# Gated products reordered across four engines, and probabilities scaled by VectorE instead of GpSimd, in a two-layer fp32 transformer kernel

## The chip, the core and the metric

The kernel runs on one core of a Trainium2 chip. The metric is the device time of one launch in microseconds (us). "Before" was timed three times. The engines go by the profile's names: PE (TensorE), DVE (VectorE), ACT (ScalarE), POOL (GpSimd), SP (SyncE, which here only issues DMAs).

## The reference

Eight sequences of 256 rows and 256 columns pass through one cross-attention over a context and then through a block of two layers, `x + tanh(g) * block(layernorm(x))`. One layer of the block, cut to what matters:

```
h = shift_token(x); q, k, v = split(h @ wqkv)          # 8 heads of 64
q, k = rotary_xpos(l2norm(q) * qs, l2norm(k) * ks)
sim  = (8 q) @ k.T over windows of 128 (own and previous), masked
o    = softmax(sim) @ v;  x = x + o @ wo
h = layernorm(shift_token(x)) * lg + lb
a, g = split(h @ w1 + b1)                               # 682 columns each
x = x + (a * gelu(g)) @ w2 + b2
```

All is fp32. Products with weights are made of three fp32r matmuls each, high by high, high by low and low by high part, so every right-hand tensor is split: a rounded copy (`u_hi`), and the remainder (`u_lo = u - u_hi`).

## The kernel before

After a first part (the cross-attention of the eight sequences, about the first 130 us) come 17 steps, s = 0 to 16. Step s does the attention of sequence-layer s and, in the same instruction streams, the feed-forward of sequence-layer s - 1; step 0 has attention only, step 16 feed-forward only. Steps 0 to 7 take layer 0, steps 8 to 15 layer 1; steps 0 and 8 also prepare weights and hold 44 narrow matmuls (L517). Each engine runs an order written out by hand, and counting semaphores tie the engines together; nothing is reordered at run time.

The feed-forward of a step has HC = 6 column chunks (5 of 128 and one of 42). For chunk c: PE `up(c)`; ACT `gelu(c)` (L830, L833); DVE `gated(c)` multiplies to `u_full[c % 4]` (L1139, semaphore `u_raw`); ACT `high_u(c)` rounds it (L839, `u_high`), but the last chunk's rounding is DVE's `high_last_u` (L1147), which waits until ACT has rounded the other five and then counts on the same semaphore; POOL `low_u(c)` forms the remainder (L1352, `u_done`). PE `down(n)`, n = 0 to 11 (two row tiles of six chunks), is the product with w2; the first six wait for `u_done`. Between chunks 3 and 4 POOL also adds the offset b2 to x1 (L1394, `xb_done`), which DVE reads only at L1260, late in the step.

The attention of a step, for each of eight heads: PE scores (L594, L600); DVE `row_min` (mask and row minimum, two instructions of 128x128 and 128x256, L1158); ACT `exps` (two ACTIVATEs with row sums, L858); DVE `row_sum` (reciprocal, L1164, `rl_done`); POOL `normalise` (two TENSOR_SCALARs over `pr`, L1370, `pn_done`); PE `tr_probs` (three transposes, L609 to L611); ACT `probs_T` (L864); PE `weighted` for each pair of heads (L623, L627); ACT `heads_out` (L869) and DVE `low_oT` (L1151). PE then transposes the next input (L415), finishes `down` and multiplies by wo (L422).

Earlier in the step DVE sums squares (`norms`, L1082), forms the low part of the feed-forward's input (`low_hT`, L1130), which `up(0)` waits for, and turns queries and keys (L1096 to L1126); POOL takes inverse square roots (L1341) and adds keys (L1346).

Before the first exponential of a step ACT loads another table (L922). In program order ACT does `gelu(4)`, `keys_T(1)`, `high_u(3)`, `gelu(5)`, the table load, `high_u(4)`, `exps(0)`, `exps(1)`; DVE does `gated(5)`, `high_last_u`, `row_min(0)`, `row_min(1)`, `row_sum(0)`, `row_min(2)`; PE does the first pair's scores, five downs, the second pair's scores, `tr_probs(0)`.

Of the kernel before, what the change touches and what calls it, by code (L numbers as in the profile page):

```python
# [18 lines left out]
P = 128  # L19
# [10 lines left out]
HEADS, DH = 8, 64  # L30
# [19 lines left out]
def build(nc, x, ctx_in, mask, g_xattn, g_ffn, Wq, bq, Wk, bk, Wv, bv, ln_gamma, ln_beta,  # L50
# [25 lines left out]
    with st:  # L76
# [99 lines left out]
        zeros_set, nhalf_set, tanh_done, prep_done = sem("zeros_set"), sem("nhalf_set"), sem("tanh_done"), sem("prep_done")  # L176
        touch_set, q1_done = sem("touch_set"), sem("q1_done")
        dve_passed, pool_passed = sem("dve_passed"), sem("pool_passed")
# [229 lines left out]
        def _(pe):  # L408
# [113 lines left out]
            def step(s, la, lf):  # L522
# [174 lines left out]
                if A:  # L697
# [8 lines left out]
                    for h in range(HEADS + 1):  # L706
                        if h in (0, 1, 3):
                            scores_own((h + 3) // 2)
                            scores_both((h + 3) // 2)
                        if h < HEADS:  # L710
                            tr_probs(h)
                        if isinstance(s, int) and s in (0, NB) and h == HEADS - 1:
                            bias_products(la)
                        downs(5 + min(5, (5 * h + 7) // 8))
                        if h and h % 2 == 0:
                            weighted(h // 2 - 1)
# [24 lines left out]
        def _(act):  # L741
# [68 lines left out]
            def step(s, la, lf):  # L810
# [100 lines left out]
                if lf is not None:  # L911
                    high_u(1)
                    gelu(3)
                    high_u(2)
                    gelu(4)
                if la is not None:
                    keys_T(1)
                if lf is not None:
                    high_u(3)
                    gelu(5)  # L920
                if la is not None:
                    A(table_touch[:, 1:2], table_touch[:, 0:1], ACT.Exp)  # L922
                if lf is not None:
                    high_u(4)
                if la is not None:
                    exps(0)
                    exps(1)
                    for h in range(HEADS):
                        if h + 2 < HEADS:
                            exps(h + 2)  # L930
                        if h >= 3 and h % 2:
                            heads_out((h - 3) // 2)
                        probs_T(h)
                    heads_out(PAIRS - 1)
                    if not (isinstance(s, int) and s == STEPS - 1):
                        evac_yT(s + 2)
# [7 lines left out]
        def _(dve):  # L944
# [131 lines left out]
            def step(s, la, lf):  # L1076
# [66 lines left out]
                def high_last_u():  # L1143
                    c, r = HC - 1, hrows[HC - 1]
                    dve.wait_ge(u_raw, HC * s)
                    dve.wait_ge(u_high, HC * s - 1)
                    V.tensor_copy(u[0][0:r, c, :], u_full[c % 4][0:r, :]).then_inc(u_high, 1)  # L1147

# [11 lines left out]

                def row_sum(h):
                    dve.wait_ge(e_done, T * (HEADS * s + h + 1))
                    wait(dve, pn_done, T * HEADS * s)
                    V.reciprocal(rl[:, h, :], ls[:, h, :]).then_inc(rl_done, 1)  # L1164

                A, F = la is not None, lf is not None
# [31 lines left out]
                if A:  # L1198
# [3 lines left out]
                    norms(1, 0)  # L1202
                    norms(1, 1)
                if F:
                    low_hT()
                if A:
                    scale_heads(0)
                    rotate_cos(1)
# [27 lines left out]
                if A:  # L1236
                    row_min(0)
                    row_min(1)
                    row_sum(0)
                    row_min(2)  # L1240
                    if start:
                        normalise_mid(NB - 1)
                    for h in range(HEADS):
                        if h + 1 < HEADS:
                            row_sum(h + 1)
                        if h + 3 < HEADS:
# [33 lines left out]
        def _(pool):  # L1280
# [51 lines left out]
            def step(s, la, lf):  # L1332
# [16 lines left out]
                def low_u(c):  # L1349
                    pool.wait_ge(u_high, HC * f + c + 1)  # L1350
                    r = hrows[c]
# [10 lines left out]
                def low_w2(l):  # L1362
                    for i, (full, high, low) in enumerate(pieces(l, False)[0:LAST_W2 - FIRST]):
                        pool.wait_ge(w_high, PIECES * l + FIRST + i + 1)
                        G.tensor_tensor(low, full, high.bitcast(F32), ALU.subtract).then_inc(w2_ready, 1)

                def normalise(h):
                    wait_apart(pool, pool_passed, (rl_done, HEADS * s + h + 1))
                    for t, (a, b) in enumerate(((0, P), (P, 3 * P))):
                        G.tensor_scalar(pr[:, h % NS, a:b], pr[:, h % NS, a:b], rl[:, h, t:t + 1], 1.0,  # L1370
                                        ALU.mult, ALU.mult).then_inc(pn_done, 1)

# [13 lines left out]
                if start:  # L1386
                    context_rstd(NB - 1)
                    rstd_x(2, NB - 1)
                if lf is not None:
                    for c in range(HC):  # L1390
                        if c == HC - 2:
                            pool.wait_ge(x1_done, s)
                            wait(pool, res_done, f)
                            G.tensor_tensor(x1b, x1[:], b2_bc[lf][:].unsqueeze(1).to_broadcast([P, T, D]),  # L1394
                                            ALU.add).then_inc(xb_done, 1)
                        low_u(c)
                if la is not None:
                    for h in range(HEADS):
                        normalise(h)
                if isinstance(s, int) and s in (0, NB):  # L1400
# [57 lines left out]
```

## Time and profile before

| what | value |
|---|---|
| median of the runs (range) | 833.61 us (833.32 to 834.94) |
| the profiled execution's own time | 832.07 us |
| its span, first to last instruction | 830.3 us |
| busy share PE, DVE, ACT, POOL | 88%, 65%, 58%, 53% |
| mean granted TensorE clock | 0.956 of full |
| one middle step (window 363.8 to 405.0 us), busy PE / DVE / ACT / POOL | 38.05 / 26.46 / 26.89 / 24.06 us of 41.2 |
| chain that ended last, share of the span | PE 46%, ACT 11%, DVE 11%, issue 10%, POOL 5% |

The chain follows the last instruction back to what released each one. PE is the busiest engine, but its modelled ends overlap, and its share says nothing of a single stretch: what a step can save is read from the waits inside it.

### The profile page before, as it was taken

How to read it: one execution, taken by the hardware profiler on the slowest of the kernel's cores; microseconds unless marked ns; L12 is line 12 of the kernel's file. 1: busy time of each engine (PE TensorE's matmuls, PEld its weight loads, DVE VectorE, ACT ScalarE, POOL GpSimd, SP SyncE). 2: the span in 40 equal slices, each digit the busy share in tenths (PEclk: the TensorE clock that was granted, in tenths of full speed). 3: DMA queues.
4: the chain of work that ended last, by engine and by line, in shares of the span. 5: the costliest groups of instructions: out<-in, count | busy, mean ns of one | idle time of the engine just before them, and what ended most of it. 6: DMA issues, size and time to landing. Idle time of an engine off the chain costs nothing.

```text
span 830.3 us, 17109 instructions
## 1 busy us (share of the span) xinstructions
PE 730.6 (88%) x4984; PEld 607.8 (73%) x4984; DVE 535.6 (65%) x1486; ACT 482.2 (58%) x1289; POOL 436.6 (53%) x592
## 2 busy tenths in 40 slices
PE   6898676989998989898988998899989899999867
PEld 5787554877777777777776877777777777777746
DVE  2899895384747474747575836666666666666632
ACT  2333424465757575757576655756575757575642
POOL 0433553473738383838382736747373737474622
PEclk9999975899999999999999988999999999999988
DMA  6444323261010101010101001010101010101000
GB/s 212 147 139 144 120 45 106 58 221 39 1 39 0 38 0 38 0 38 0 38 0 39 1 1 51 3 51 0 51 0 51 0 51 0 51 0 39 2 26 13
DMA packets 32786, 38.36 MB, mean 46 GB/s; under 512 B 8476, under 2 KB 22896, under 8 KB 32752
## 3 DMA queue, kind: packets, MB, share of 16 engines
q1 hardware_dynamic: 32752, 37.95, 14.2%
q8 instruction: 16, 0.26, 0.1%
q14 instruction: 18, 0.15, 0.1%
HBM read 29.55 MB, written 8.39 MB: 46 GB/s over the span
## 4 chain that ended last, share of the span: by engine, by line
PE 46%; ACT 11%; DVE 11%; issue 10%; POOL 5%; DVEq 1%; ACTq 0%; POOLq 0%
PE ps L422 26%; PE ps L623 4%; ACT pr L858 4%; PE ps L582 3%; ACT L922 2%; PE ps L609 2%; PE ps L600 2%; PE ps L594 2%; DVE ss L1082 2%; DVE turned L1096 2%; POOL rn L1341 1%; PE ps L627 1%; ACT pT L864 1%; POOL pr L1370 1%; PE ps L415 1%
## 5 line engine op out<-in xcount | busy, mean ns | idle before, releaser
L1370 POOL TENSOR_SCALAR pr<-pr,rl 128x128 f32<-128x128 f32 (+1 forms) x256 | 107.0, 430 | 78.7 <-DVE rl L1164 78.0
L858 ACT ACTIVATE pr<-sm,mn 128x128 f32<-128x128 f32 (+1 forms) x256 | 113.4, 445 | 30.2 <-DVE mn L1158 30.1
L422 PE MATMUL ps<-hT_hi,w_hi 128*128 128x256 f32 (+1 forms) x352 | 105.3, 299 | 5.4 <-DVE hT_lo L1130 5.4
L1158 DVE CUSTOM_DVE_ANT_0 sm<-ps,wmask 128x128 f32<-128x128 f32 (+1 forms) x256 | 79.9, 354 | 45.2 <-PE ps L600 39.9
L422 PE MATMUL ps<-hT_hi,w_lo 128*128 128x256 f32 (+1 forms) x352 | 100.4, 285 | 0.0
L422 PE MATMUL ps<-hT_lo,w_hi 128*128 128x256 f32 (+1 forms) x352 | 99.5, 283 | 0.0
L1341 POOL TENSOR_TENSOR rn<-ss,nhalf 128x16 f32<-128x16 f32 x32 | 96.7, 3022 | 2.7
L818 ACT ACTIVATE sqb<-ps 128x512 f32<-128x512 f32 x64 | 38.0, 595 | 95.0 <-PE ps L422 88.3
L422 PE MATMUL ps<-wqkv_hi,yT_hi 128*128 128x512 f32 x192 | 80.0, 417 | 7.7 <-DVE arena L1002 5.2
L1286 POOL TENSOR_SCALAR hrs<-hmv 128x2 f32<-128x2 f32 x16 | 3.1, 192 | 152.9 <-DVE hmv L1181 152.9
L1352 POOL TENSOR_TENSOR u_lo<-u_pair,u_hi 128x256 fp32r<-128x256 f32 x64 | 70.9, 1116 | 23.4 <-ACT u_hi L839 22.7
L422 PE MATMUL ps<-w_hi,u_hi 128*128 128x256 f32 x192 | 66.3, 345 | 16.6 <-POOL u_lo L1352 16.5
L422 PE MATMUL ps<-wqkv_lo,yT_hi 128*128 128x512 f32 x192 | 77.1, 402 | 0.0
L422 PE MATMUL ps<-wqkv_hi,yT_lo 128*128 128x512 f32 x192 | 77.0, 401 | 0.0
L422 PEld LDWEIGHTS ps<-hT_hi,w_hi 128*128 128x128 f32 (+1 forms) x352 | 66.9, 190 | 12.5 <-DVE hT_lo L1130 12.4
L830 ACT ACTIVATE gl<-ps,b_sb 128x256 f32<-128x256 f32 x80 | 37.9, 474 | 56.4 <-PE ps L422 55.4
L864 ACT ACTIVATE pT<-ps 128x384 f32<-128x384 f32 x128 | 61.5, 482 | 11.9 <-PE ps L611 10.5
L422 PEld LDWEIGHTS ps<-hT_lo,w_hi 128*128 128x128 f32 (+1 forms) x352 | 67.2, 191 | 0.0
L422 PEld LDWEIGHTS ps<-hT_hi,w_lo 128*128 128x128 f32 (+1 forms) x352 | 66.6, 189 | 0.0
L609 PE MATMUL ps<-ident,pr 128*128 128x128 f32 x128 | 42.2, 330 | 23.1 <-POOL pr L1370 21.8
L1151 DVE TENSOR_TENSOR oT_lo<-ps,oT_hi 128x256 fp32r<-128x256 f32 x64 | 27.1, 423 | 49.7 <-ACT oT_hi L869 48.1
L609 PEld LDWEIGHTS ps<-ident,pr 128*128 128x128 f32 x128 | 18.2, 142 | 52.8 <-POOL pr L1370 44.8
(150 smaller groups left out, 2137.5 us busy)
## 6 DMA issues: line engine op xcount, KB each, us to landing
arena<-x SPq DMA_DIRECT2D x16, 256.0 KB, 3.4
ystream<-arena SPq DMA_DIRECT2D x16, 256.0 KB, 2.0
y_next<-ystream SPq DMA_DIRECT2D x16, 256.0 KB, 2.8
y_res<-ystream SPq DMA_DIRECT2D x16, 256.0 KB, 2.7
arena<-L_ffn_w SPq DMA_DIRECT2D x6, 640.0 KB
arena<-ctx SPq DMA_DIRECT2D x8, 256.0 KB, 3.7
arena<-mask_BxSxS_ik SPq DMA_DIRECT2D x8, 256.0 KB, 2.7
xmid<-arena SPq DMA_DIRECT2D x8, 256.0 KB, 2.0
```

The costliest lines, as they stand in the source:

```text
L422: last = mm(out, lhsT(a), rhs(b), start=(start and i == 0), stop=(stop and i == 2))
L609: nc.tensor.transpose(b[:, 0:P], p[:, 2 * P:3 * P], ident[:])
L623: mm(b[j * DH:(j + 1) * DH, 0:S], vs[:, 0, h * DH:(h + 1) * DH], pT[:, h % 4, P:3 * P], start=True, stop=False)
L818: A(sqb[:, j * INNER:(j + 1) * INNER], bank(i + j), ACT.Square).then_inc(sq_done, 1)
L830: A(gl[:, c % 2, :], ps[:, 5 + c % 2, S:2 * S], ACT.Gelu, bias=b1_sb[:, lf, 1, c:c + 1]).then_inc(gl_done, 1)
L858: A(pr[:, h % NS, a:b], sm[:, h % NS, a:b], ACT.Exp, bias=mn[:, h, t:t + 1], scale=-1.0, accum_out=ls[:, h, t:t + 1]).then_inc(e_done, 1)
L864: A(pT[:, h % 4, :], bank(3 + h % 2)[:, 0:3 * P], ACT.Copy).then_inc(pT_done, 1)
L1151: V.tensor_tensor(oT[1][:, pair, :], bank(5 + pair % 2)[:, 0:S], oT[0][:, pair, :].bitcast(F32), ALU.subtract).then_inc(o_done, 1)
L1158: V.tensor_tensor_reduce(sm[:, h % NS, a:b], bank(h % SB)[:, a:b], wmask[:, a:b], 1.0, -NEG, ALU.add, ALU.min, mn[:, h, t:t + 1]).then_inc ...
L1341: G.tensor_tensor(rn[:, t, :], ss[:, t, :], nhalf[:], ALU.pow).then_inc(rn_done, 1)
L1352: G.tensor_tensor(u[1][0:r, c, :], u_full[c % 4][0:r, :], u[0][0:r, c, :].bitcast(F32), ALU.subtract).then_inc(u_done, 1)
L1370: G.tensor_scalar(pr[:, h % NS, a:b], pr[:, h % NS, a:b], rl[:, h, t:t + 1], 1.0, ALU.mult, ALU.mult).then_inc(pn_done, 1)
```

## The change

On DVE the reciprocal of the row sums is followed at once by the two multiplications of `pr`, and `normalise` leaves POOL. `high_last_u` no longer waits for ACT and has a semaphore of its own, `u_last`. ACT rounds chunks 3 and 4 before `gelu(5)` and the table load. POOL adds b2 after all six `low_u`. PE does two more downs ahead of `tr_probs(0)` and spreads the rest otherwise. On DVE `low_hT` moves ahead of the fourth `norms`. The diff without its line numbers and unchanged surroundings:

```diff
 # tensor
+                        if h == 0:
+                            downs(7)
                         if h < HEADS:
                             tr_probs(h)
...
-                        downs(5 + min(5, (5 * h + 7) // 8))
+                        downs(min(10, 7 + (h + 1) // 2))
 # scalar
                     gelu(4)
+                    high_u(3)
                 if la is not None:
                     keys_T(1)
                 if lf is not None:
-                    high_u(3)
+                    high_u(4)
                     gelu(5)
                 if la is not None:
                     A(table_touch[:, 1:2], table_touch[:, 0:1], ACT.Exp)
-                if lf is not None:
-                    high_u(4)
-                if la is not None:
                     exps(0)
 # vector, high_last_u
                     dve.wait_ge(u_raw, HC * s)
-                    dve.wait_ge(u_high, HC * s - 1)
-                    V.tensor_copy(...).then_inc(u_high, 1)
+                    V.tensor_copy(...).then_inc(u_last, 1)
-                def row_sum(h):
+                def scale_by_sum(h):
                     dve.wait_ge(e_done, T * (HEADS * s + h + 1))
-                    wait(dve, pn_done, T * HEADS * s)
                     V.reciprocal(rl[:, h, :], ls[:, h, :]).then_inc(rl_done, 1)
+                    dve.wait_ge(rl_done, HEADS * s + h + 1)
+                    for t, (a, b) in enumerate(((0, P), (P, 3 * P))):
+                        V.tensor_scalar(pr[:, h % NS, a:b], pr[:, h % NS, a:b], rl[:, h, t:t + 1], None,
+                                        ALU.mult).then_inc(pn_done, 1)
...
                     norms(1, 0)
+                if F:
+                    low_hT()
+                if A:
                     norms(1, 1)
-                if F:
-                    low_hT()
-                if A:
                     scale_heads(0)
 # vector, the loop over heads: row_sum becomes scale_by_sum in both places
 # gpsimd
                 def low_u(c):
-                    pool.wait_ge(u_high, HC * f + c + 1)
+                    if c < HC - 1:
+                        pool.wait_ge(u_high, (HC - 1) * f + c + 1)
+                    else:
+                        pool.wait_ge(u_last, s)
...
-                def normalise(h):
-                    wait_apart(pool, pool_passed, (rl_done, HEADS * s + h + 1))
-                    for t, (a, b) in enumerate(((0, P), (P, 3 * P))):
-                        G.tensor_scalar(pr[...], pr[...], rl[...], 1.0, ALU.mult, ALU.mult).then_inc(pn_done, 1)
...
                 if lf is not None:
                     for c in range(HC):
-                        if c == HC - 2:
-                            (wait x1_done, res_done; add b2 to x1)
                         low_u(c)
+                    add_offset()      # the same wait and addition
-                if la is not None:
-                    for h in range(HEADS):
-                        normalise(h)
```

## Rows read from the trace of the kernel before

**Rows 1.** timeline of PE, step 6: start, us, engine, line, operation [idle <-releaser]

```profile
377.66 0.38 PE L422 MATMUL ps<-hT_hi,w_hi 128*128 128x256 f32 x1 [0.23 <-DVE hT_lo L1130]
...
390.99 0.38 PE L422 MATMUL ps<-w_hi,u_hi 128*128 128x256 f32 x1 [1.03 <-POOL u_lo L1352]
...
391.54 0.49 PE L594 MATMUL ps<-kT,qT 64*128 64x128 f32 x4
...
393.54 0.33 PE L609 MATMUL ps<-ident,pr 128*128 128x128 f32 x1 [1.08 <-POOL pr L1370]
...
402.11 0.65 PE L623 MATMUL ps<-pT,vs 128*64 128x256 f32 x4 [0.18 <-DVE oT_lo L1151]
```

**Rows 2.** timeline of ACT, step 6

```profile
389.52 0.20 ACT L922 ACTIVATE table_touch<-table_touch 128x1 f32<-128x1 f32 x1
...
391.09 0.40 ACT L858 ACTIVATE pr<-sm,mn 128x128 f32<-128x128 f32 x1 [1.06 <-DVE mn L1158]
...
393.36 0.40 ACT L858 ACTIVATE pr<-sm,mn 128x128 f32<-128x128 f32 x1 [0.41 <-DVE mn L1158]
...
397.25 0.40 ACT L858 ACTIVATE pr<-sm,mn 128x128 f32<-128x128 f32 x1
...
398.72 0.49 ACT L864 ACTIVATE pT<-ps 128x384 f32<-128x384 f32 x1 [0.22 <-PE ps L611]
...
401.50 0.95 ACT L864 ACTIVATE pT<-ps 128x384 f32<-128x384 f32 x2
```

**Rows 3.** timeline of POOL, step 6

```profile
388.47 1.28 POOL L1394 TENSOR_TENSOR arena<-x,b_bc 128x512 f32<-128x512 f32 x1
390.11 1.51 POOL L1352 TENSOR_TENSOR u_lo<-u_pair,u_hi 128x256 fp32r<-128x256 f32 x2 [0.35 <-ACT u_hi L839]
392.66 1.78 POOL L1370 TENSOR_SCALAR pr<-pr,rl 128x128 f32<-128x128 f32 x4 [1.04 <-DVE rl L1164]
```

**Rows 4.** timeline of DVE, step 6

```profile
386.44 0.48 DVE L1139 SCALAR_TENSOR_TENSOR u_pair<-ps,b_sb,gl 128x256 f32<-128x256 f32 x1 [0.94 <-ACT gl L830]
...
388.24 0.48 DVE L1139 SCALAR_TENSOR_TENSOR u_pair<-ps,b_sb,gl 42x256 f32<-42x256 f32 x1 [0.72 <-ACT gl L833]
390.06 0.28 DVE L1147 CAST u_hi<-u_pair 42x256 fp32r<-42x256 f32 x1 [1.34 <-ACT u_hi L839]
...
392.19 0.17 DVE L1164 RECIPROCAL rl<-ls 128x2 f32<-128x2 f32 x1 [0.58 <-ACT pr L858]
392.68 0.29 DVE L1158 CUSTOM_DVE_ANT_0 sm<-ps,wmask 128x128 f32<-128x128 f32 x1 [0.32 <-PE ps L600]
...
393.24 0.16 DVE L1164 RECIPROCAL rl<-ls 128x2 f32<-128x2 f32 x1
```

**Rows 5.** groups of DVE by line and shape: xcount, busy us, mean ns, idle before

```profile
L960 DVE TENSOR_SCALAR arena<-arena,xmv,xrs 128x256 f32<-128x256 f32 x48 | 22.5, 510 | 9.6 <-POOL xrs L1288 9.5
...
L970 DVE TENSOR_SCALAR arena<-ps,xrl 128x256 f32<-128x256 f32 x16 | 7.0, 476 | 0.0
...
L1059 DVE TENSOR_SCALAR gam_bc<-gam_bc,tg 128x256 f32<-128x256 f32 x1 | 0.3, 334 | 0.0
```

**Rows 6.** timeline of DVE, step 1

```profile
183.99 0.85 DVE L1147 CAST u_hi<-u_pair 42x256 fp32r<-42x256 f32 x1 [1.42 <-ACT u_hi L839]
```

**Rows 7.** timeline of POOL, step 1

```profile
183.96 0.72 POOL L1352 TENSOR_TENSOR u_lo<-u_pair,u_hi 128x256 fp32r<-128x256 f32 x1 [0.35 <-ACT u_hi L839]
```

**Rows 8.** busy time and granted clock of PE, stretches of steps 8, 10 and 15

```profile
core 0: us, PE busy (x), PEclk, DMA share, GB/s
480.10:487.00 6.90, 6.47 (x31) 0.51 0.00 0
575.70:579.10 3.40, 3.40 (x16) 0.50 0.00 0
783.90:787.30 3.40, 3.40 (x18) 0.50 0.00 0
```

**Rows 9.** timeline of PE, last step

```profile
822.72 0.39 PE L422 MATMUL ps<-w_hi,u_hi 128*128 128x256 f32 x1 [1.34 <-POOL u_lo L1352]
```

More of the change, by code:

```diff
@@ L176, in build @@
         zeros_set, nhalf_set, tanh_done, prep_done = sem("zeros_set"), sem("nhalf_set"), sem("tanh_done"), sem("prep_done")
-        touch_set, q1_done = sem("touch_set"), sem("q1_done")
+        touch_set, q1_done, u_last = sem("touch_set"), sem("q1_done"), sem("u_last")
         dve_passed, pool_passed = sem("dve_passed"), sem("pool_passed")
@@ L1145, in high_last_u @@
                     dve.wait_ge(u_raw, HC * s)
-                    dve.wait_ge(u_high, HC * s - 1)
-                    V.tensor_copy(u[0][0:r, c, :], u_full[c % 4][0:r, :]).then_inc(u_high, 1)
+                    V.tensor_copy(u[0][0:r, c, :], u_full[c % 4][0:r, :]).then_inc(u_last, 1)
                 def low_oT(pair):
@@ L1202, in step @@
                     norms(1, 0)
-                    norms(1, 1)
                 if F:
@@ L1206, in step @@
                 if A:
+                    norms(1, 1)
                     scale_heads(0)
@@ L1238, in step @@
                     row_min(1)
-                    row_sum(0)
+                    scale_by_sum(0)
                     row_min(2)
@@ L1244, in step @@
                         if h + 1 < HEADS:
-                            row_sum(h + 1)
+                            scale_by_sum(h + 1)
                         if h + 3 < HEADS:
@@ L1365, in low_w2 @@
                         G.tensor_tensor(low, full, high.bitcast(F32), ALU.subtract).then_inc(w2_ready, 1)
-                def normalise(h):
-                    wait_apart(pool, pool_passed, (rl_done, HEADS * s + h + 1))
-                    for t, (a, b) in enumerate(((0, P), (P, 3 * P))):
-                        G.tensor_scalar(pr[:, h % NS, a:b], pr[:, h % NS, a:b], rl[:, h, t:t + 1], 1.0,
-                                        ALU.mult, ALU.mult).then_inc(pn_done, 1)
                 if lf is not None:
@@ L1388, in step, with add_offset @@
                     rstd_x(2, NB - 1)
+                def add_offset():
+                    pool.wait_ge(x1_done, s)
+                    wait(pool, res_done, f)
+                    G.tensor_tensor(x1b, x1[:], b2_bc[lf][:].unsqueeze(1).to_broadcast([P, T, D]),
+                                    ALU.add).then_inc(xb_done, 1)
                 if lf is not None:
                     for c in range(HC):
-                        if c == HC - 2:
[L1392 to L1395, printed above, removed]
                         low_u(c)
-                if la is not None:
-                    for h in range(HEADS):
-                        normalise(h)
+                    add_offset()
                 if isinstance(s, int) and s in (0, NB):
```

## The prediction, made before the changed kernel was run

> **What bounds the kernel now.** I read the page first: PE is 88% busy, yet only 46% of the chain that ended last is PE's; the rest is handed about between ACT, DVE, POOL and issue. The time is thus in hand-overs between engines. A middle step takes 41.2 us, and its neighbours look alike, so one step read closely counts fifteen times (steps 1 to 15 hold every edit; steps 0 and 16 some). Next I took the waits of one middle step and looked only at those where PE stands, then the timelines of the four engines from the last gated product on.
>
> In PE's timeline of step 6 two stalls stand out [rows 1]: 1.03 us before the fifth down (390.99), released by POOL's `u_lo`, and 1.08 us before the first transposed probabilities (393.54), released by POOL's scaled `pr`. Later ones are small. The 0.18 us at 402.11 is named after DVE's `oT_lo`; but that `weighted` needs only the first `low_oT`, long done. What it waits for is `probs_T(5)`, the first of the two ACTIVATEs at 401.50 [rows 2], which ends near 401.97: there the bound is ACT.
>
> Behind the first stall is POOL's queue [rows 3]: it adds b2 from 388.47 for 1.28 us while the fourth remainder could be formed, and the last two take 1.51 us from 390.11. Behind the second stall is a longer chain. DVE finishes the last gated product at 388.24 + 0.48 = 388.72, then waits 1.34 us in `high_last_u` for ACT's `high_u(4)`, which stands behind the table load; `row_min(0)` waits behind it in DVE's queue [rows 4]. So ACT, free at 389.72, idles 1.06 us before its first exponential [rows 2]. The reciprocal starts at 392.19 [rows 4], POOL at 392.66 [rows 3], PE at 393.54 [rows 1]: 1.35 us from reciprocal to PE.
>
> **The change part by part.**
>
> *The last rounded chunk.* `high_last_u` has to wait only for its own engine. A hand-over from ACT to PE took 402.11 - 401.97 = 0.14 us [rows 1, 2], one to itself lies between nothing and that; I take 0.04, so it starts at 388.76 instead of 390.06: 1.30 us earlier. ACT then has what it needs at 391.09 - 1.30 = 389.79, and it is free at 389.72 with `high_u(4)` out of the way [rows 2, 4]. So the first exponential gains 1.30 us. `high_u(4)` now lies ahead of `gelu(5)`, in place of `high_u(3)`, which moves into an ACT gap before `keys_T(1)`: cost nothing in steps 1 to 15, because the moved instruction takes the slot of the one that left.
>
> *The order of POOL and PE.* The fifth remainder no longer lies behind the addition (1.28 us) nor behind the table load. It takes the place of the fourth, which ended by 388.47, when the addition began [rows 3]; PE wants it at 390.99 - 1.03 = 389.96 [rows 1]: the 1.03 us stall goes. The sixth starts behind the CAST of 388.76 + 0.28 and takes 0.75, so ends near 389.8, and the addition near 391.1; its reader L1260 comes after the whole head loop. PE puts two downs (at most 391.54 - 390.99 = 0.55 us each) where the second stall was; the transposes behind them are wanted only after `exps(2)`, so they stay covered. The number of downs is unchanged; those two are taken from places behind `tr_probs(1)` and `tr_probs(2)`.
>
> *Scaling on DVE.* No row shows a 128x128 or 128x256 scaling of `pr` by DVE. The nearest is L1059, a multiplication of 128x256 by one column, SBUF to SBUF, at 334 ns; the same form out of PSUM, L970, takes 476 ns; L960, two columns and 256 elements, has a mean of 510 ns that includes waits [rows 5]. I take 334 ns for the wide one. Since 476 - 334 = 142 ns for 256 elements is about half their streaming time, the narrow one has some 70 ns less: 264 ns. With the reciprocal (0.17) and a self-wait (0.04) a `scale_by_sum` takes 0.17 + 0.04 + 0.26 + 0.33 = 0.80 us at most, 0.77 with a little overlap. Bounds: 0.75 (the overlap of neighbouring DVE instructions full) and 0.17 + 0.04 + 2 x 0.51 = 1.23 (both at L960's mean). From reciprocal to PE the hand-over falls from 1.35 to about 0.9 us.
>
> The cost is that `row_min(h + 2)` stands behind `scale_by_sum(h)` on DVE. Walk it: reciprocal at 392.19 - 1.30 = 390.89, scaling done at 391.66, `row_min(2)` there instead of 392.68: 1.02 us earlier. PE doesn't hold it: scores of the second pair, started at 391.54 before, gave `row_min(2)` 1.14 us later [rows 1, 4]; without the first stall they start near 390.3. `exps(2)` gains the same 1.02 us. From there a head costs DVE 0.77 + 0.56 (393.24 - 392.68) = 1.33 us [rows 4], and ACT (397.25 - 393.36) / 3 = 1.30 us [rows 2]: a tie, in which DVE can lose about 0.1 us over the heads. Back comes ACT's 0.22 us before `probs_T(3)` [rows 2], because PE is by then further ahead. Together the pair that was at 402.11 starts 1.02 - 0.05 + 0.2 = about 1.2 us earlier, and behind it PE's order is the same as before, so 1.2 us is what the step gains here. The stalls removed are larger (1.03 + 1.08 = 2.11); the difference, 0.9 us, returns as new short idles of PE in the second half of the head loop, where ACT and DVE set the pace.
>
> *`low_hT` one instruction earlier.* `up(0)` waits 0.23 us for it [rows 1], but ACT's high part is ready only about when `norms` ends, so it gains 0.06 us. `scale_heads(0)` comes 0.23 us later; DVE's next idle, 0.94 us before `gated(4)`, absorbs it [rows 4]. Without that cover it would cost 0.23 us a step.
>
> *A shared path between DVE and POOL.* In step 1 the CAST took 0.85 us instead of 0.28 while POOL's `u_lo`, started 0.03 us before, ran 0.72 us [rows 6, 7]; the rest of the profile has the 0.28 [rows 4]. Such a hold could strike the first scaling (390.9 + 0.2 = 391.1) if the b2 addition still ran; by the walk it ends at 391.1, so I count nothing, at most 0.3 us a step. Later heads meet an idle POOL. The Trainium skill, in "SBUF — State Buffer", section "SBUF: two separate sides", says the pair of ports shared by VectorE and GpSimd is locked by whichever starts first for its whole instruction, and VectorE needs it in a two-port mode. This case's rows 6 and 7 agree (0.85 against 0.28 us); by that rule the sum would be unchanged unless the two meet, and then 0.3 us a step less.
>
> *Ends.* Step 0 has the scaling alone: 0.5 us. In the last step PE waits 1.34 us behind the addition [rows 9]; the fifth remainder comes 1.3 us sooner, but the sixth is now behind a later `gelu(5)`; between 0 and 1.34 I take 0.7.
>
> **Sum.** 15 x (1.2 + 0.06) + 0.5 + 0.7 = 20.1 us. Against the profiled execution, 832.07 - 20.1 = 812.0; its time lies 1.5 us under the median of the runs, so 833.6 - 20.1 = 813.5 us, a gain of 2.4%.
>
> **Rivals.**
>
> *The clock goes with the stalls.* After the second stall the granted clock was 0.50 (1.2 GHz) in stretches of 3.4, 3.4 and about 6.9 us in steps 10, 15 and 8 [rows 8], where the engine had stood at the same two places as in [rows 1] shortly before. Elsewhere that place ran at 2.4 GHz with the same stalls. At most half of 13.7 us, 6.8 us, is lost there. If denser work kept the clock up, up to 6 us more are won: 807.5. Against it: new idles arise near the end of the head loop, and the fall may move there. The Trainium skill, "TensorE: Matmul & The Clock Gate", section "HAM oscillation — how this bites in real kernels", says that idling of PE brings the slow clock back; rows 8 don't contradict it, and by it this rival gives the same 807.5.
>
> *DVE costs more, half the gain.* Each 0.1 us more on `scale_by_sum` costs up to 0.6 us a step over six heads. At 0.87 us (no overlap, later hand-overs) the gain is 1.26 - 0.6 = 0.66, in all 11 us: 822.5. If instead the addition on POOL holds the first scaling, 0.96 a step: 818. Together the case spans 817 to 826. For it: the tie of 1.33 to 1.30 leaves no slack.
>
> *DVE becomes the bound and the kernel slower.* One mechanism: `row_min(h + 2)` waits in DVE's queue behind `scale_by_sum(h)`, and the exponentials behind it. It decides where `scale_by_sum` exceeds 0.77 + 1.26 / 6 = 0.98 us. At the PSUM form's speed (0.48 and 0.34) it would be 1.03 and the time about as before or 4 us above; at L960's mean, 1.23, six heads lose 6 x 0.46 = 2.8 us, the step is 1.5 us longer and the time 833.6 + 15 x 1.5 - 1.2 = 855. Against it: the edit reads SBUF and one column, as L1059 does, not PSUM or two columns [rows 5], and POOL is idle in the loop.
>
> *Nothing changes.* Had another wait, such as the last `low_oT` before wo, held the step, the gains would stop there. It follows `weighted(3)` and moves with it. So only a `scale_by_sum` of just 0.98 us gives no change.
>
> **How the numbers follow.** Chances: forecast, 809 to 817, 0.50; clock rival, 804 to 809, 0.17; half the gain, 817 to 826, 0.20 (three quarters of it under 822); below 804, 0.04; no change, 0.04 within 0.2% (1.7 us, about what this measurement can tell); slower 0.05. Range 804 to 822: 0.50 + 0.17 + 0.15 = 0.82. Faster 0.91, same 0.04, slower 0.05.
>
> **What would show it.** Right: no PE wait on `u_lo` before the fifth down; the CAST directly behind the last gated product; DVE scalings near 0.26 and 0.33 us; `exps(0)` 0.1 us after the table's touch; steps 39.9 us apart. Wrong: scalings of 0.5 us, ACT waiting for `row_min` in every head, DVE's CAST or first scaling lengthened beside POOL, or a clock of 0.5 in the head loop of more steps than three.

## The result, and the profile after

The changed kernel takes 803.63 us (median of four runs, 801.82 to 805.47) against 834.28 us in the runs of the kernel before that were made with them: a ratio of 0.9628, 95% interval 0.9597 to 0.966, so 3.7% or 30.6 us faster. The forecast was 813.5 us; the range (804 to 822) was missed at its low end by 0.4 us, which is less than the four runs differ among themselves. The profiled execution took 804.17 us, span 802.3. Busy shares are now PE 90%, DVE 74%, ACT 60%, POOL 41%, and PE holds 52% of the chain that ended last instead of 46%.

Step 6 again, as in [rows 1 to 4]. First PE (start, us, engine, line, operation, idle before and who ended it):

```profile
388.67 0.27 PE L609 MATMUL ps<-ident,pr 128*128 128x128 f32 x1
...
391.79 0.65 PE L623 MATMUL ps<-pT,vs 128*64 128x256 f32 x4 [0.44 <-ACT pT L866]
...
396.63 0.33 PE L609 MATMUL ps<-ident,pr 128*128 128x128 f32 x1 [0.33 <-DVE pr L1165]
397.42 0.65 PE L623 MATMUL ps<-pT,vs 128*64 128x256 f32 x4 [0.24 <-ACT pT L866]
...
399.42 0.65 PE L623 MATMUL ps<-pT,vs 128*64 128x256 f32 x4 [0.66 <-ACT pT L866]
```

The stalls of 1.03 and 1.08 us [rows 1] are gone: no wait stands before any down, none before the first transposed probabilities (388.67). What is left are four small ones, the largest 0.66 us. ACT in the same step:

```profile
386.27 0.20 ACT L925 ACTIVATE table_touch<-table_touch 128x1 f32<-128x1 f32 x1
386.54 0.40 ACT L860 ACTIVATE pr<-sm,mn 128x128 f32<-128x128 f32 x1
...
388.90 0.40 ACT L860 ACTIVATE pr<-sm,mn 128x128 f32<-128x128 f32 x1 [0.49 <-DVE mn L1157]
```

The first exponential follows the table's touch without a wait (1.06 us before [rows 2]). The third still waits 0.49 us for its minimum. Why, DVE shows:

```profile
384.99 0.48 DVE L1139 SCALAR_TENSOR_TENSOR u_pair<-ps,b_sb,gl 42x256 f32<-42x256 f32 x1 [0.71 <-ACT gl L835]
385.50 0.29 DVE L1146 CAST u_hi<-u_pair 42x256 fp32r<-42x256 f32 x1
385.86 0.29 DVE L1157 CUSTOM_DVE_ANT_0 sm<-ps,wmask 128x128 f32<-128x128 f32 x1
...
387.56 0.17 DVE L1162 RECIPROCAL rl<-ls 128x2 f32<-128x2 f32 x1 [0.50 <-ACT pr L860]
387.76 0.55 DVE L1165 TENSOR_SCALAR pr<-pr,rl 128x128 f32<-128x128 f32 x2
388.23 0.28 DVE L1157 CUSTOM_DVE_ANT_0 sm<-ps,wmask 128x128 f32<-128x128 f32 x1
...
389.44 0.28 DVE L1157 CUSTOM_DVE_ANT_0 sm<-ps,wmask 128x128 f32<-128x128 f32 x1
...
390.65 0.28 DVE L1157 CUSTOM_DVE_ANT_0 sm<-ps,wmask 128x128 f32<-128x128 f32 x1
```

The rounding (L1146) stands right behind the last gated product, where it waited 1.34 us before [rows 4]. Reciprocal and both scalings take 388.23 - 387.56 = 0.67 us, and `row_min(2)` stands behind them. From there DVE's cycle is 390.65 - 389.44 = 1.21 us a head. The scalings by shape (xcount, busy us, mean ns, idle before), to set beside [rows 5]:

```profile
L1165 DVE TENSOR_SCALAR pr<-pr,rl 128x256 f32<-128x256 f32 x128 | 44.5, 348 | 0.0
L1165 DVE TENSOR_SCALAR pr<-pr,rl 128x128 f32<-128x128 f32 x128 | 36.8, 287 | 4.5
```

POOL forms the last two remainders as soon as each rounded chunk is there, and adds b2 behind them, where [rows 3] had it in front:

```profile
384.54 0.72 POOL L1357 TENSOR_TENSOR u_lo<-u_pair,u_hi 128x256 fp32r<-128x256 f32 x1 [0.26 <-ACT u_hi L841]
385.87 0.73 POOL L1357 TENSOR_TENSOR u_lo<-u_pair,u_hi 42x256 fp32r<-42x256 f32 x1 [0.60 <-DVE u_hi L1146]
386.56 1.27 POOL L1392 TENSOR_TENSOR arena<-x,b_bc 128x512 f32<-128x512 f32 x1
```

The last step keeps half of its stall (1.34 us in [rows 9]):

```profile
795.47 0.39 PE L422 MATMUL ps<-w_hi,u_hi 128*128 128x256 f32 x1 [0.67 <-POOL u_lo L1357]
```

The whole span, cut where PE begins each step's L415 transposes (distances in us, worked out from PE's timelines of three profiles; "again" is the kernel before profiled once more, the last experiment):

| stretch | before | before again | changed |
|---|---|---|---|
| start to step 0 | 154.34 | 157.97 | 159.46 |
| 0 to 1 | 44.49 | 44.53 | 42.57 |
| each from 2 to 7, mean of 5 | 41.17 | 41.47 | 39.64 |
| 7 to 8 (layer change) | 54.67 | 54.54 | 47.89 |
| 8 to 9 | 45.20 | 45.43 | 44.28 |
| 9 to 10 | 42.55 | 41.24 | 39.64 |
| each from 10 to 14, mean of 4 | 41.22 | 41.56 | 39.64 |
| 14 to PE's last instruction | 72.77 | 72.21 | 67.99 |

A middle step without slow clock went from 41.17 to 39.64 us, 1.53 less where 1.26 was forecast. The first row, which ends with step 0, is mostly chance: ahead of step 0 nothing was changed, and four of the experiments built on the changed kernel have 154.4 to 154.8 us there. In steps 0, 1, 8, 9 and the last, slow-clock stretches fall in all three profiles, so these rows mix the change with the clock.

### The profile page after: what moved, and what is told of

It is laid out like the page before. It is cut to its first block, busy times and chain, and to the rows that moved or that the text cites. A ratio compares the mean times of both kernels' runs of the same rounds, so it can differ in the third digit from the quotient of the medians.

```text
span 802.3 us, 16737 instructions
## 1 busy us (share of the span) xinstructions
PE 722.3 (90%) x4984; PEld 602.4 (75%) x4984; DVE 595.5 (74%) x1742; ACT 481.1 (60%) x1289; POOL 330.3 (41%) x336
## 4 chain that ended last, share of the span: by engine, by line
PE 52%; ACT 14%; DVE 7%; issue 6%; POOL 2%; DMA 1%; ACTq 0%; SPq 0%; DVEq 0%; POOLq 0%
PE ps L422 36%; ACT pr L860 7%; PE ps L623 4%; PE ps L582 3%; ACT pT L866 3%; PE ps L517 2%; PE ps L600 2%; DVE sm L1157 2%; PE ps L415 1%; PE ps L594 1%; PE ps L627 1%; DVE hT_lo L1130 1%; ACT hT_hi L899 1%; ACT oT_hi L871 1%; DVE w_lo L1039 1%
## 5 line engine op out<-in xcount | busy, mean ns | idle before, releaser
L1165 DVE TENSOR_SCALAR pr<-pr,rl 128x128 f32<-128x128 f32 (+1 forms) x256 | 70.4, 317 | 4.5
L422 PE MATMUL ps<-w_hi,u_hi 128*128 128x256 f32 x192 | 62.8, 327 | 0.7 <-POOL u_lo L1357 0.7
L623 PE MATMUL ps<-pT,vs 128*64 128x256 f32 x256 | 42.7, 412 | 19.2 <-ACT pT L866 19.2
L422 PE MATMUL ps<-w_hi,u_lo 128*128 128x256 f32 x192 | 54.1, 282 | 0.0
```

The source lines that it names most:

```text
L422: last = mm(out, lhsT(a), rhs(b), start=(start and i == 0), stop=(stop and i == 2))
L623: mm(b[j * DH:(j + 1) * DH, 0:S], vs[:, 0, h * DH:(h + 1) * DH], pT[:, h % 4, P:3 * P], start=True, stop=False)
L1165: V.tensor_scalar(pr[:, h % NS, a:b], pr[:, h % NS, a:b], rl[:, h, t:t + 1], None, ALU.mult).then_inc(pn_done, 1)
```

## Experiments

Each ratio is to runs of the kernel before on the same chip in the same session (medians 833.2 to 835.0 us). A "step" below is the distance of two middle steps in the profile; these distances repeat within some 0.02 us.

### The parts one by one

**The scaling alone.** The kernel before, with the reciprocal and scalings on DVE as in the change:

```diff
-                            row_sum(h + 1)
+                            scale_by_sum(h + 1)
...
-                        normalise(h)
```

> The kernel before, with one part of the change: DVE multiplies the probabilities right behind its reciprocal, POOL's normalise is gone; the order of roundings, remainders and downs is the old one. Theory A (the hand-overs around the last gated product set the step, and the scaling's place is off the path there): PE's stall before the first transposed probabilities shrinks from 1.08 us to about 0.5, but ACT's first exponential starts no earlier, so the step gains 0 to 0.3 us and the kernel lands at 829 to 834 us. Theory B (the long way over POOL was the main cost): the step gains its 0.6 us or more and the kernel lands at 820 to 825 us.

Measured: 828.73 us, ratio 0.9926 (0.9892 to 0.9959), close to theory A's range. The five runs form two groups, 823.9 and 824.2 us, and 828.7 to 830.1; the profile is of the fastest. The step is 41.01 us, only 0.16 less, and PE's two stalls of step 6 read:

```profile
389.89 0.39 PE L422 MATMUL ps<-w_hi,u_hi 128*128 128x256 f32 x1 [1.03 <-POOL u_lo L1355]
391.83 0.33 PE L609 MATMUL ps<-ident,pr 128*128 128x128 f32 x1 [0.46 <-DVE pr L1166]
```

The first stands, the second has shrunk from 1.08 to 0.46 us. Fifteen steps of 0.16 us make 2.4 of the 6.2 us; the rest is put down to stretches that lost a slow clock (below).

**The order alone.** The changed kernel with the two scalings back on POOL. With `row_sum` an old wait of DVE ahead of its reciprocal is back too, which the change had removed:

```diff
+                    wait(dve, pn_done, T * HEADS * s)
```

> The changed kernel with one part undone: POOL scales again, behind the b2 addition. Theory A: the first exponential keeps its 1.3 us and row_min(2) has no scaling before it on DVE, so the step gains 1.1 to 1.4 us and the kernel lands at 808 to 815 us, the clock's dips in the head loop gone with the two stalls. Theory B: most of the gain goes with the scaling, 822 us or more.

Measured: 801.89 us, ratio 0.9616 (0.9595 to 0.9637), step 39.55, faster than either theory had it. The order carries all of the gain; the scaling on DVE adds 0.09 us to a step. The intervals of this kernel and the changed one overlap. ACT's first exponential and DVE's first reciprocal of one step:

```profile
381.61 0.40 ACT L860 ACTIVATE pr<-sm,mn 128x128 f32<-128x128 f32 x1
```

```profile
382.72 0.17 DVE L1163 RECIPROCAL rl<-ls 128x2 f32<-128x2 f32 x1 [0.59 <-ACT pr L860]
```

The reciprocal starts 1.11 us behind the exponential, as before the change (392.19 - 391.09 = 1.10 in [rows 2, 4]). In the changed kernel it is 387.56 - 386.54 = 1.02 us, and so it is with the scaling alone. The distance is 1.11 us in the four profiles that have the wait and 1.02 us in the eight that don't and keep DVE's order. That the wait, though long fulfilled, costs the 0.09 us is likely and not shown: the kernels with it are also those where POOL scales.

**The old rounding.** The changed kernel, with ACT's order and the wait of the last rounding as before:

```diff
-                    high_u(3)
                 if la is not None:
                     keys_T(1)
                 if lf is not None:
+                    high_u(3)
                     gelu(5)
                 if la is not None:
                     A(table_touch[:, 1:2], table_touch[:, 0:1], ACT.Exp)
+                if lf is not None:
+                    high_u(4)
...
+                    dve.wait_ge(u_high, ...)
```

> The changed kernel, but ACT rounds chunk 3 after keys_T(1) and chunk 4 behind the table load, and DVE's last rounding waits for ACT's five, as before. Theory A: the first exponential comes 1.0 to 1.3 us later than in the changed kernel and PE stands 0.9 us before the fifth down, so the step is 1.0 to 1.4 us longer: 818 to 826 us, with slow-clock stretches back in some steps. Rival: the other parts cover it, under 810 us.

Measured: 828.7 us, ratio 0.9929 (0.9903 to 0.9956), step 41.28, which is 1.64 more than with the edit and more than the 1.0 to 1.4 expected. PE waits 0.93 to 1.03 us on `u_lo` in every step again, but the slow clock did not come back in the head loops of the profile. This edit carries the gain; without it the other parts together leave a step 0.1 us longer than before. The run undoes ACT's order and DVE's wait together and does not tell the two apart.

**The old place of the b2 addition**, ahead of the fifth remainder:

> The changed kernel, but POOL adds b2 before the fifth remainder again (1.28 us). Theory A: with the roundings early, the fifth remainder ends at about the time PE wants it (386.5 us in the changed kernel's middle step), so at most 0.2 us a step is lost in steps 1 to 15, and 0.7 us in the last step: 803 to 807 us. Rival (the addition's place is worth its own 1.28 us less nothing): the step is 0.7 us or more longer, 814 us or more.

Measured: 811.28 us, ratio 0.9723 (0.9697 to 0.975), step 40.04, 0.39 more. Expected was at most 0.2, by way of a late remainder. But PE does not wait for it; another line changed. DVE and POOL of step 6:

```profile
386.33 0.85 DVE L1146 CAST u_hi<-u_pair 42x256 fp32r<-42x256 f32 x1
```

```profile
385.06 1.28 POOL L1392 TENSOR_TENSOR arena<-x,b_bc 128x512 f32<-128x512 f32 x1
386.29 0.74 POOL L1357 TENSOR_TENSOR u_lo<-u_pair,u_hi 128x256 fp32r<-128x256 f32 x1
```

The addition pushes the fifth remainder onto the moment of DVE's rounding, 0.04 us ahead of it, and the rounding takes 0.85 us instead of 0.29. That is the pair of [rows 6, 7], now in every step (0.48 us in the last, 0.68 and 0.70 in steps 1 and 8, 0.85 in the others). `row_min(0)` and all exponentials come some 0.4 us later. The last step's stall on `u_lo` is 1.33 us again. The Trainium skill, "SBUF — State Buffer", section "SBUF: two separate sides", gives the rule (whichever of the two starts first holds the shared ports for its whole instruction); this case's rows agree, 0.85 against 0.29 us.

The kernel before had this pair more often than the prediction took from [rows 6, 7]: the rounding took 0.85 us in steps 1, 8 and 15 and 1.15 us in the last one. Step 15 and the last step:

```profile
779.79 0.84 DVE L1147 CAST u_hi<-u_pair 42x256 fp32r<-42x256 f32 x1 [1.41 <-ACT u_hi L839]
...
820.93 1.15 DVE L1147 CAST u_hi<-u_pair 42x256 fp32r<-42x256 f32 x1
```

In the changed kernel all sixteen take 0.28 or 0.29 us. So the change also removed three such pairs from whole steps; at the 0.39 us that one costs here, they are worth some 1.2 us in all, an estimate.

**The old place of `low_hT`:**

> The changed kernel with the lower half of the transposed activations taken after VectorE's second norm again, as before. By the prediction the move is worth 0.06 us a step. Theory A: 0.05 to 0.15 us a step more, 804.4 to 806 us. Theory B (TensorE's wait for it in the first group of the first product is not on the path, as TensorE waits for others later in the step): no change, 803.6 us.

Measured: 804.68 us, ratio 0.9656 (0.964 to 0.9672), step 39.71: 0.07 more, where 0.06 was forecast. The intervals of the two medians overlap; the step shows it.

**The old spread of the downs:**

> The changed kernel with one thing put back: how many groups of the second product stand ahead of each head's work in TensorE's order. Before, one group came ahead of transposing head 1's probabilities and the rest were spread over heads 0 to 4 by (5h + 7)/8; the changed kernel puts two ahead of head 0's transposes. Theory A: the groups are only filler, the sum of TensorE's work is the same, and they matter where TensorE waits for the probabilities of the head. In the changed kernel it waits 0.44, 0.24 and 0.66 us ahead of three of the weighted sums; fewer groups ahead of head 0 would lengthen the first of these and shorten a later one: 0 to +0.3 us for each of 16 steps, 803 to 808 us. Theory B (the new split is what fills the wait for the first probabilities and so carries part of the gain of 1.6 us a step): +0.5 to +0.8 us a step, 811 to 816 us, with a wait of at least 0.8 us ahead of head 0's transposes.

Measured: 803.49 us, ratio 0.9621 (0.9589 to 0.9653), step 39.64: nothing. The 0.44 us idle moves from ahead of the first weighted sum to ahead of head 0's transposes. The downs are filler; neither place is on the path.

### What holds the third exponential

**The minimum of head 2 ahead of the first scaling:**

```diff
                     row_min(1)
-                    scale_by_sum(0)
                     row_min(2)
+                    scale_by_sum(0)
```

> The changed kernel, but VectorE takes the row minimum of head 2 ahead of the first reciprocal and its two scalings. ScalarE idles 0.49 us ahead of head 2's exponential in the changed kernel, because that minimum stands behind 0.67 us of reciprocal and scalings. Theory A (what VectorE does late is all that delays it): the minimum starts 0.67 us earlier, ScalarE's idle time goes, and as ScalarE's cycle sets the pace of the head loop, each step is 0.4 to 0.5 us shorter: 796 to 797 us. Theory B (the scores of head 2 are what comes next): TensorE writes them only at about 388.15 in step 6, 0.1 us before the minimum starts now, so the minimum gains 0.1 us, and the scaling of head 0 comes up to 0.6 us later: within 0.1 us a step, 802 to 805 us.

Measured: 810.54 us, ratio 0.971 (0.9683 to 0.9738), step 40.04. Both expectations were wrong; it costs 0.39 us a step. DVE, then PE:

```profile
386.74 0.29 DVE L1157 CUSTOM_DVE_ANT_0 sm<-ps,wmask 128x128 f32<-128x128 f32 x1 [1.08 <-PE ps L600]
```

```profile
388.10 0.33 PE L609 MATMUL ps<-ident,pr 128*128 128x128 f32 x1 [0.67 <-DVE pr L1165]
```

DVE stands 1.08 us waiting for the scores, with the finished exponential of head 0 behind that wait. The third exponential gains less than 0.1 us, and the scaling comes so late that PE waits 0.67 us for it, and the copies `probs_T` wait behind PE.

**The same, with the scores of the second pair one group of the second product earlier**, `downs(4)` for `downs(5)`:

> As the run before, and TensorE does four instead of five groups of the second product before the scores of heads 2 and 3 (one group is about 0.55 us), so that the scores are there when VectorE can take their minimum. Theory A (ScalarE's 0.49 us of idle time before head 2's exponential is what is left on the path at the start of the head loop, and both the scores and the place on VectorE hold it): 0.4 to 0.5 us a step less than the changed kernel, 796 to 798 us, with no wait of ScalarE before that exponential. Theory B (TensorE is full by now, and the time comes back as waits behind the weighted sums): no change, 802 to 805 us.

Measured: 804.0 us, ratio 0.9626 (0.96 to 0.9652), step 39.68. The earlier scores give back what the new order cost and no more.

**Earlier scores in the changed kernel:**

> The changed kernel with four instead of five groups of the second product before the scores of heads 2 and 3 and nothing else. With the reordering alone this took 0.2 us off each step. Theory A (in the changed kernel VectorE is not free when these scores come: it is in the reciprocal and scalings of head 0 until 388.23 of step 6, and earlier scores gain no more than the 0.1 us by which they were late): 802 to 804 us. Theory B (TensorE's order is what limits both): 0.2 us a step less, 799 to 801 us.

Measured: 801.52 us, ratio 0.9609 (0.9586 to 0.9631), step 39.64: no change in the step; DVE is in head 0's scaling until then.

**Earlier scores with the order alone** (POOL scales):

> The reordering alone (POOL scales the probabilities, VectorE does the reciprocals only), with four instead of five groups of the second product before the scores of heads 2 and 3. Without scalings VectorE reaches the minimum of head 2 early and waits for the scores. Theory A: the minimum comes one group (0.55 us) earlier, ScalarE's idle time before head 2's exponential goes, 0.3 to 0.5 us a step: 794 to 797 us against 801.9 for the reordering alone. Theory B (TensorE full, or POOL's scaling as late as the weighted sums): no change, 801 to 803 us.

Measured: 797.51 us, ratio 0.956 (0.9534 to 0.9586), step 39.35, and ACT's wait before the third exponential of step 6 is 0.22 us:

```profile
382.42 0.40 ACT L860 ACTIVATE pr<-sm,mn 128x128 f32<-128x128 f32 x1 [0.22 <-DVE mn L1157]
```

It is the fastest kernel of the study, though the step gained 0.2 us where theory A had 0.3 to 0.5. With POOL scaling, DVE is free when the scores come, so earlier scores count (3 us in all); with DVE scaling they don't.

### The slower rival: VectorE as the bound

Each scaling cut into pieces of 64 columns, six instructions for two, the same result:

```diff
-                        V.tensor_scalar(pr[:, h % NS, a:b], pr[:, h % NS, a:b], rl[:, h, t:t + 1], None,
-                                        ALU.mult).then_inc(pn_done, 1)
+                        for c in range(a, b, DH):
+                            last = V.tensor_scalar(pr[:, h % NS, c:c + DH], pr[:, h % NS, c:c + DH],
+                                                   rl[:, h, t:t + 1], None, ALU.mult)
+                        last.then_inc(pn_done, 1)
```

> The changed kernel with each head's two scalings cut into six of 64 columns each, so that VectorE's part of the head loop gets about 0.4 to 0.5 us longer for each head (a 64-column scaling is taken as about 0.17 to 0.2 us in sequence; no trace shows one), the result the same. This tests the slower rival of the prediction, VectorE as the bound of the head loop. Theory A (VectorE's cycle of 1.21 us a head now stands just under ScalarE's 1.25, so any more is paid in nearly every head): cycle 1.6 to 1.7 us, for 6 to 8 heads 2.4 to 3.6 us a step, 842 to 861 us. Theory B (TensorE, at 90% of the span, has slack at the end of the head loop that absorbs it): under 0.5 us a step, 804 to 811 us.

Measured: 849.05 us, ratio 1.0212 (1.0166 to 1.0258): slower than before the change, by 1.7 to 2.6%. DVE, and PE's waits, of one middle step:

```profile
358.18 0.16 DVE L1162 RECIPROCAL rl<-ls 128x2 f32<-128x2 f32 x1
358.37 1.07 DVE L1166 TENSOR_SCALAR pr<-pr,rl 128x64 f32<-128x64 f32 x6
359.36 0.28 DVE L1157 CUSTOM_DVE_ANT_0 sm<-ps,wmask 128x128 f32<-128x128 f32 x1
```

```profile
361.23 0.33 PE L609 MATMUL ps<-ident,pr 128*128 128x128 f32 x1 [0.83 <-DVE pr L1166]
...
368.48 0.33 PE L609 MATMUL ps<-ident,pr 128*128 128x128 f32 x1 [1.16 <-DVE pr L1166]
```

`scale_by_sum` is now 359.36 - 358.18 = 1.18 us, 0.51 more, and the step 42.28 us, 2.64 more: the price of 5.2 heads. On a straight line through these two points, an estimate, the step would be back at 41.17 us with a block of 0.67 + 1.53 / 5.2 = 0.96 us.

### The clock

The kernel before once more, unchanged:

> The kernel before once more, unchanged, to see whether the stretches at 1.2 GHz in its head loops come back in the same steps. Theory A (they follow from the instruction stream: the 1.03 us and 0.7 to 0.9 us waits of TensorE in front of and inside the head loop together): a granted clock of 0.5 in the head loops of steps 8, 10 and 15 again, and a step of 54 us between steps 7 and 8. Theory B (chance of one execution): other steps or none, and times that differ by the 3 to 4 us that such a stretch costs.

Measured: 836.83 us, a single execution. Granted clock (in the last three columns: clock, DMA share, GB/s) of four slow stretches and, last, of the place in step 10 that was slow in [rows 8]; before these columns stand the window, its length and the busy time (instructions) of PE, PE's weight loads, DVE, ACT and POOL:

```profile
356.70:359.90 3.20, 3.20 (x17) 2.55 (x17) 1.46 (x10) 2.24 (x9) 1.54 (x5) 0.51 0.00 0
486.20:489.40 3.20, 3.20 (x17) 2.39 (x16) 1.39 (x11) 2.08 (x9) 1.50 (x4) 0.50 0.00 0
499.80:506.60 6.80, 6.80 (x34) 5.87 (x35) 0.59 (x4) 0.38 (x1) 2.82 (x2) 0.50 0.00 0
663.70:666.90 3.20, 3.20 (x17) 2.22 (x15) 1.29 (x9) 2.20 (x10) 1.56 (x4) 0.50 0.00 0
579.60:583.00 3.40, 2.39 (x21) 1.50 (x17) 2.00 (x14) 2.98 (x13) 2.34 (x6) 1.00 0.00 0
```

The third begins in the 44 narrow matmuls (L517, 496.9 to 503.6 us) of step 8; the others are in head loops again, but of steps 5, 8 and 12 instead of 8, 10 and 15. Step 8 is in both; the others differ between two executions of one program. Where one fell, the step took 42.64 or 42.55 us instead of 41.2, so one such stretch costs 1.4 us, not the 3 to 4 us expected. The split scaling, with stalls of 0.83 and 1.16 us in every head loop, has them too, running from one step into the next; one of its two:

```profile
411.40:418.00 6.60, 5.94 (x30) 4.14 (x29) 2.17 (x8) 2.30 (x5) 0.00 (x0) 0.50 0.00 0
```

None of the eleven profiles whose middle steps have at most one stall of 0.8 us or more (the changed kernel and all other experiments) shows 1.2 GHz in a head loop of steps 1 to 15 ahead of L517. That is one profile of each kernel. In the changed kernel step 8's head loop runs at full clock:

```profile
474.00:486.00 12.00, 11.16 (x98) 9.03 (x97) 6.49 (x32) 7.51 (x28) 0.00 (x0) 1.00 0.01 2
```

Two kernels tell the clock from the waits. With the old rounding a middle step is 0.11 us longer than before, yet the kernel is about 6 us faster: 4.3 of it between steps 7 and 8, 1.3 between 9 and 10 and 2.2 behind step 14, where slow stretches had been in [rows 8]. Of the 2.2 us, 0.7 is the last step's stall on `u_lo`, now two of 0.31 and 0.32 us instead of 1.34. The 6.2 us of the medians, less this 0.7, plus 15 x 0.11 = 1.6 for the longer steps, leave some 7 us for the clock. With the scaling alone 3.8 us are left beyond the steps' 2.4.

The mean granted clock of all runs gives a bound: a run at a mean share c of full speed lost at most (1 - c) of its span. The medians are 36.7 us for the kernel before, 29.4 with the old rounding, 31.4 with the scaling alone and 32.0 for the changed kernel, each within some 0.4 us for the last digit of c. So the clock gave back at most 7.3, 5.3 and 4.7 us. The first two agree with what is left above. So one stall fewer of the two was enough in the two profiles, and in the medians it goes with 4 to 7 us. That the stalls bring the slow clock is inferred from where it appears; no run changes the one without the other.

## Why the prediction came out as it did

**Right about the waits.** The first exponential, counted from the first pair's scores, came 2.37 us behind them instead of 3.67 (386.54 - 384.17, and 391.09 - 387.42 before): 1.30 us earlier, as forecast. Both stalls went; the rounding follows the gated product at once; part of the stalls' 2.11 us came back as small waits in the head loop; `low_hT` gave 0.07 us in its own run where 0.06 was forecast. In the last step 1.34 - 0.67 = 0.67 us were won where 0.7 was taken. The break-even of `scale_by_sum`, given as 0.98 us, is 0.96 by the line through the split scaling, whose block of 1.18 us gave 849 us.

**The sum's mis-sized term.** Two steps of the prediction failed: this one, and the clock, which the sum put at nothing (below). The first is "*Walk it: ... `row_min(2)` there instead of 392.68: 1.02 us earlier*", with what follows from it, "*a tie, in which DVE can lose about 0.1 us*", so that "*1.2 us is what the step gains here*". `scale_by_sum` was taken as 0.77 us and measured 0.67, below its lower bound of 0.75. The single instructions were longer than taken (287 and 348 ns for 264 and 334), but the pair takes 0.55 us, not their sum of 0.64, and the next instruction starts 0.47 us behind the pair's start: DVE starts an instruction before the last one's recorded end, and 0.03 us was allowed for this. This makes 0.10 us. Another 0.09 goes with the wait on `pn_done` that the diff removes ahead of the reciprocal: the walk moved the reciprocal by the exponential's 1.30 us alone, but it starts 1.02 us behind the exponential instead of 1.11. So the third exponential gained 1.21 us instead of 1.02, and DVE's cycle is 1.21 us where 1.33 was worked out, just under ACT's 1.25: no tie, no loss. Behind it ACT's wait of 0.22 us went as forecast.

How far the start of the third exponential carries the step is seen across the runs (step 6 of each):

| kernel | third exponential behind first scores | middle step |
|---|---|---|
| before | 5.94 | 41.17 |
| scaling alone | 6.03 | 41.01 |
| old rounding | 6.38 | 41.28 |
| old b2 place | 5.13 | 40.04 |
| changed; old downs | 4.73 | 39.64; 39.64 |
| order alone | 4.64 | 39.55 |
| order, four downs | 4.46 | 39.35 |

In the last five rows, which share the front part of the step, the step differs by what the exponential does, within 0.02 us. The two rows above add 0.07 to 0.09 us in front, where `low_hT` has its old place, and the kernel before also some 0.23 behind. The orders with `row_min(2)` first are the exception: there the first scaled probabilities are the later of the two.

**What the forecast attributed to the scaling.** The forecast named a hand-over from reciprocal to PE falling from 1.35 to about 0.9 us. With the scaling alone it fell to 0.81 us, and 0.46 us of stall was left where 1.08 was, but nothing waits for it once the downs cover it; the two runs with one part each show the scaling at -0.16 us a step on the old order and +0.09 on the new. The gain is from the earlier roundings (1.64 us a step when taken away) and from keeping POOL's addition off it (0.39).

**The clock: a rival that should have been a term.** "*The clock goes with the stalls.*" was priced at up to 6 us and given as another outcome, chance 0.17. It is no alternative to the shorter waits: the stalls that go are the ones in front of [rows 8], and both came, so it belonged in the sum. What the runs showed in place of nothing is a gain of at most 4.7 us for the changed kernel, by the granted clock. "*New idles arise near the end of the head loop, and the fall may move there*" did not happen; idles of 0.24 to 0.66 us did not bring the slow clock. The account of medians: forecast 20.1, plus 15 x (1.53 - 1.26) = 4.0 for the steps, plus some 1.2 for the rounding beside POOL in steps 1, 8 and 15, plus at most 4.7 for the clock, makes at most 30.0 us of the 30.6 measured. With either the steps or the clock alone the time would have been in the range.

**A reading that was wrong.** "*the rest of the profile has the 0.28*" holds for steps 2 to 7 and 9 to 14, not for steps 8, 15 and the last. The prediction counted what the changed kernel might lose by such a hold, and not what the kernel before was losing already.

**Not seen, or open.** The 0.5 us of step 0 can't be told: the stretch up to it varies by 5 us between executions of kernels that are alike there. The layer change took 47.9 us in the changed kernel's profile and 48.9 to 51.6 in those of the experiments with ACT's new order and whole scalings; how slow stretches fall there is chance as far as these runs show. Why the pair of stalls brings the slow clock in some steps and not in others was not found. In steps 1, 8 and 15 of the kernel before, where the rounding took 0.85 us, the second stall is 1.34 us; the fall came in step 8 in both profiles, in step 15 in one and in step 1 in none.

## What to carry to other kernels

When an engine waits, look first at what stands queued behind the waiting instruction: here a cheap rounding of 42 columns waited for work of another engine that it did not need, and the whole head loop stood behind it. Moving work from a slow engine to a faster one was worth next to nothing (0.16 us a step in the old order, a loss of 0.09 in the new), because the slow one was off the path; the fastest version leaves it there and uses the freed place to bring the scores forward. And where slow-clock stretches lie just behind the stalls that an edit removes, add their price to the sum. Before calling a contention rare, look at every step's instance of the instruction, not at one step and its neighbour.

## What the runs showed of the hardware

- Two DVE multiplications by a column, 128 and 256 elements, SBUF to SBUF, are recorded as 287 and 348 ns, yet take 0.55 us together; six of 64 elements (mean 249 ns) take 1.07 us. The extra 128 elements cost 61 ns, 0.48 ns each, while the masked minimum, which reads PSUM and a mask in SBUF, takes 286 and 420 ns, 1.05 ns for each. The Trainium skill, "VectorE: DVE Perf Modes", section "The perf-mode tier table", gives a scaling from SBUF in fp32 twice the rate of a two-input operation; these rows agree (a factor of 2.2), though the minimum reads PSUM besides.
- A DVE rounding of 42x256 started 0.04 us behind a POOL subtraction of 128x256 takes 0.85 us instead of 0.29, and cost 0.39 us in a middle step.
- A DVE instruction can start before the recorded end of the one before it: the two scalings end at 387.76 + 0.55 = 388.31, and the minimum behind them starts at 388.23.
- Slow-clock stretches of 3.4 us in a head loop cost 1.4 us of time in a middle step, and fell in other steps from one execution of a program to the next.
